# Cross-attention on one core: values of alternate head groups moved within their strip, output projection by two full products

## What is computed

```python
q = proj(hs, Wq, bq, S)          # 32 x 16 heads x 56 x 16
k = proj(at, Wk, bk, T)          # 32 x 16 heads x 1500 x 16
v = proj(at, Wv, bv, T)
scores = jnp.einsum('bhsd,bhtd->bhst', q, k) / scale
...
probs = jax.nn.softmax(scores, axis=-1)
ctx = jnp.einsum('bhst,bhtd->bhsd', probs, v)
ctx = ctx.transpose(0, 2, 1, 3).reshape(B, S, H)
delta = ctx @ Wo.T + bo
```

## Time and profile before

| | us |
|---|---|
| median of 3 runs | 1445.63 (1444.37 to 1446.39) |
| the profiled execution | 1444.34 |
| its span, first to last instruction | 1442.4 |
| PE busy | 1376.7 (95%) |
| PEld busy | 1176.8 (82%) |
| DVE busy | 1013.8 (70%) |
| ACT busy | 716.9 (50%) |
| POOL busy | 447.3 (31%) |

### The profile page before, as it was taken

One profiled execution on the slowest core, in us unless ns is written; L12 is line 12 of the kernel. 1 busy time (PEld: TensorE's weight loads), 2 busy tenths in 40 slices (PEclk: granted clock), 3 DMA queues, 4 the chain that ended last, 5 costly groups with the idle time before them and its releaser, 6 DMA issues.

```text
span 1442.4 us, 54968 instructions
## 1 busy us (share of the span) xinstructions
PE 1376.7 (95%) x25094; PEld 1176.8 (82%) x25094; DVE 1013.8 (70%) x1792; ACT 716.9 (50%) x939; POOL 447.3 (31%) x400
## 2 busy tenths in 40 slices
PE   5899999998899999999999999999999999999983
PEld 5687787786688888888888888888888888888872
DVE  4676676666136787786777777687878778677765
ACT  3445445444255645555555555555554555555540
POOL 4332333222222333333324233233333333332400
PEclk9999999999899999999999999999999999999995
DMA  9100001000111121111112121111212121121100
GB/s 260 23 1 31 1 1 31 1 30 1 58 49 57 31 77 44 56 58 46 58 37 63 31 77 52 57 49 45 64 31 77 41 62 55 45 61 34 49 2 7
DMA packets 38808, 66.75 MB, mean 46 GB/s; under 512 B 3605, under 2 KB 36818, under 8 KB 38578
## 3 DMA queue, kind: packets, MB, share of 16 engines
q1 hardware_dynamic: 38578, 63.24, 15.1%
HBM read 61.40 MB, written 1.84 MB: 44 GB/s over the span
## 4 chain that ended last, share of the span: by engine, by line
PE 71%; DVE 2%; issue 0%; POOL 0%; POOLq 0%; DVEq 0%
PE proj_ps L1277 19%; PE proj_ps L1268 19%; PE score_ps L1295 14%; PE sum_ps L1315 12%; PE side_ps L1350 2%; PE side_ps L1332 2%; PE side_ps L1364 1%; PE side_ps L1357 1%; PE side_ps L1339 0%; DVE inv L1109 0%; DVE exps L1097 0%; DVE amax L1150 0%; DVE hidden L1182 0%; DVE hidden L1193 0%; DVE sig L1192 0%
## 5 line engine op out<-in xcount | busy, mean ns | idle before, releaser
L1049 ACT ACTIVATE exps<-score_ps 125x1792 f32<-125x1792 f32 x192 | 320.5, 1669 | 419.0 <-PE score_ps L1295 419.0
L1097 DVE TENSOR_SCALAR exps<-exps,top 125x896 f32<-125x896 f32 x384 | 287.9, 791 | 18.0 <-ACT exps L1049 17.5
L1295 PE MATMUL score_ps<-spread,keys 32*125 32x112 f32 x6144 | 219.3, 279 | 0.0
L1315 PEld LDWEIGHTS sum_ps<-exps,vals 125*32 125x32 f32 x12288 | 163.0, 110 | 50.9 <-issue 34.4
L1088 DVE COPY vals<-proj_ps 125x512 f32<-125x512 f32 x192 | 128.2, 687 | 103.4 <-PE proj_ps L1277 103.0
L1295 PEld LDWEIGHTS score_ps<-spread,keys 32*125 32x125 f32 x6144 | 185.1, 183 | 15.4 <-issue 0.4
L1315 PE MATMUL sum_ps<-exps,vals 125*32 125x56 f32 x12288 | 191.5, 214 | 2.9 <-DVE exps L1097 2.9
L992 POOL TENSOR_TENSOR low<-raw_early,high 128x500 fp32r<-128x500 f32 x64 | 100.8, 1583 | 231.2 <-issue 115.4
L992 POOL TENSOR_TENSOR low_early<-raw_early,high_early 128x500 fp32r<-128x500 f32 x62 | 104.3, 1691 | 172.3 <-issue 104.1
L1041 ACT ACTIVATE keys<-proj_ps,b_k 128x500 f32<-128x500 f32 x192 | 129.9, 677 | 52.4 <-PE proj_ps L1268 52.4
L286 POOL TENSOR_TENSOR swapped<-swapped,sin 128x448 f32<-128x448 f32 (+1 forms) x72 | 88.6, 1232 | 138.5 <-ACT swapped L507 138.5
(11 more groups left out here) (156 smaller groups left out, 2411.6 us busy)
## 6 DMA issues: line engine op xcount, KB each, us to landing
raw_early<-in_ctxT SPq DMA_DIRECT2D x64, 500.0 KB, 4.0
raw<-in_ctxT SPq DMA_DIRECT2D x32, 500.0 KB, 3.5
w_q<-in_attn_Wq SPq DMA_DIRECT2D x4, 512.0 KB, 8.1
w_o<-in_attn_Wo SPq DMA_DIRECT2D x1, 2048.0 KB, 21.5
out<-y_out SPq DMA_DIRECT2D x16, 112.0 KB, 1.9
rows<-in_x SPq DMA_DIRECT2D x1, 1344.0 KB, 16.8
raw_early<-in_ffn_gate_wT SPq DMA_DIRECT2D x1, 1024.0 KB, 9.6
raw_early<-in_ffn_val_wT SPq DMA_DIRECT2D x1, 1024.0 KB, 5.1
```

The lines of the kernel that those rows point to most:

```text
L1049: nc.scalar.activation(exps[t % 2][:, :, :, :].rearrange("p h r n -> p r h n"), score_ps[0:TILE, :, 0:2 * QW].rearrange("p r (h n) -> p r ...
L1097: nc.vector.tensor_scalar(tile, tile, LIMIT_LO, top[:, n, at:at + 1], ALU.max, ALU.min)\
L1295: ins = nc.tensor.matmul(score_ps[0:TILE, r, to:to + HE * S], keys[c % 2][32 * r:32 * r + 32, k, (at + half) * TILE:(at + half + 1) * TILE ...
L1315: ins = nc.tensor.matmul(sum_ps[32 * h:32 * h + VW, g, :], vals[c % 2][:, at + half, HJ * g + h, :], exps[t % 2][:, half, r, col:col + S], ...
```

## The change

For groups 1 and 3, `add_up` takes a window of `vals` that begins 16 columns earlier: the ones of the head before, then the values of its own head. Their sums of exponents then stand in the upper 16 rows of a strip (the first ones) and the weighted values in the 16 rows behind them. `divide` takes the reciprocal as before, shuffles the even groups from the second 16 rows and the odd groups from the first, multiplies all, sets the unwanted rows of the odd groups to zero with a mask column (`part`), multiplies the even groups by the other mask column and adds the odd ones, and adds the bias. So two groups share one column block of `heads`, now 128 full rows, and L1332 is two products over 128 rows in place of four, with a `w_xo` without zeros whose rows are ordered on the host. `divide` has seven instructions (and two loads of a shuffle mask) in place of four (and one), and an `EventSemaphore` instruction less; four of them work on 112 elements or less per row instead of 224. The bias and the weights come in by one DMA each and the mask by one (14 early DMAs instead of 19).

```diff
-N_EARLY = 11 + 2 * HJ
+N_EARLY = 14
...
-SWAP = [HD + n % HD for n in range(2 * HD)]
+FROM_HIGH = [HD + n % HD for n in range(2 * HD)]
+FROM_LOW = [n % HD for n in range(2 * HD)]
+DIVS = 6
...
-        self.b_v = sb("b_v", [P, HG])
-        self.w_xo = sb("w_xo", [P, HG, D])
+        self.b_v = sb("b_v", [P, HG // 2])
+        self.w_xo = sb("w_xo", [P, HG // 2, D])
+        self.part = sb("part", [P, 2])
...
-        for j in range(HJ):
-
-            pairs += [(self.b_v[32 * j:32 * j + HD, :], dram["xattn_bv"][j]),
-                      (self.w_xo[32 * j:32 * j + HD, :, :],
-                       dram["xattn_WoT"].rearrange("(a j d) n -> j d a n", a=HG, j=HJ)[j])]
+        pairs += [(self.b_v[:, :], dram["xattn_bv"]), (self.part[:, :], dram["c_part"]),
+                  (self.w_xo[:, :, :], dram["xattn_WoT"].rearrange("(a p) n -> p a n", p=P))]
...
-        heads = sb("heads", [P, HG, 2, S])
+        heads = sb("heads", [P, HG // 2, 2, S])
...
-                chain = Chain(dve, div_step, 6 * p + 3 * k)
+                chain = Chain(dve, div_step, DIVS * (2 * p + k))
                 chain(nc.vector.reciprocal(inv[:, k, :, :], sums[:, k, :, :]))
-                nc.vector.sem_inc(inv_ready, 1)
-                chain(nc.vector.stream_shuffle(inv[:, k, :, :].rearrange("p a s -> p (a s)"),
-                                               inv[:, k, :, :].rearrange("p a s -> p (a s)"), SWAP))
-                chain(nc.vector.tensor_tensor(heads[:, :, k, :], sums[:, k, :, :], inv[:, k, :, :], ALU.mult))
-                nc.vector.tensor_tensor(heads[:, :, k, :], heads[:, :, k, :],
-                                        b_v[:, :].unsqueeze(2).to_broadcast([P, HG, S]), ALU.add)\
+                chain.inc(nc.vector.stream_shuffle(inv[:, k, 0::2, :], inv[:, k, 0::2, :], FROM_HIGH))
+                chain(nc.vector.stream_shuffle(inv[:, k, 1::2, :], inv[:, k, 1::2, :], FROM_LOW))
+                chain(nc.vector.tensor_tensor(inv[:, k, :, :], sums[:, k, :, :], inv[:, k, :, :], ALU.mult))
+                chain(nc.vector.tensor_scalar(inv[:, k, 1::2, :], inv[:, k, 1::2, :], part[:, 1:2], None, ALU.mult))
+                chain(nc.vector.scalar_tensor_tensor(inv[:, k, 0::2, :], inv[:, k, 0::2, :], part[:, 0:1], inv[:, k, 1::2, :],
+                                                     ALU.mult, ALU.add))
+                assert chain.n == DIVS
+                nc.vector.tensor_tensor(heads[:, :, k, :], inv[:, k, 0::2, :],
+                                        b_v[:, :].unsqueeze(2).to_broadcast([P, HG // 2, S]), ALU.add)\
                   .then_inc(heads_ready, 1)
...
+            def value_and_ones(r, tile, head):
+
+                at = (tile * XH + head) * VW - (HD if head // HJ % 2 else 0)
+                return vals[r][:, :, :, :].rearrange("p t h v -> p (t h v)")[:, at:at + VW]
...
-                                sum_ps[32 * h:32 * h + VW, g, :], vals[c % 2][:, at + half, HJ * g + h, :],
+                                sum_ps[32 * h:32 * h + VW, g, :], value_and_ones(c % 2, at + half, HJ * g + h),
...
-                    for a in range(HG):
+                    for a in range(HG // 2):
                         ins = nc.tensor.matmul(side_ps[0:ROWS, 0:D], heads[:, a, :, :].rearrange("p k s -> p (k s)"),
-                                               w_xo[:, a, :], start=(a == 0), stop=(a == HG - 1))
+                                               w_xo[:, a, :], start=(a == 0), stop=(a == HG // 2 - 1))
...
+        "c_part": np.stack([row % (2 * HD) < HD, row % (2 * HD) >= HD], 1).astype(np.float32),
...
-        "xattn_WoT": a(L0_xattn_Wo).T, "xattn_bq": a(L0_xattn_bq).reshape(DC, P).T,
+        "xattn_WoT": a(L0_xattn_Wo).T.reshape(HG // 2, 2, HJ, HD, D).transpose(0, 2, 1, 3, 4).reshape(D, D), "xattn_bq": a(L0_xattn_bq).reshape(DC, P).T,
...
-        "xattn_bv": a(L0_xattn_bv).reshape(HG, HJ, HD).transpose(1, 2, 0), "xattn_bo": a(L0_xattn_bo), "xattn_gamma": a(L0_xattn_ln_gamma),
+        "xattn_bv": a(L0_xattn_bv).reshape(HG // 2, 2, HJ, HD).transpose(2, 1, 3, 0).reshape(P, HG // 2), "xattn_bo": a(L0_xattn_bo), "xattn_gamma": a(L0_xattn_ln_gamma),
```

More of the change, by code:

```diff
@@ L47 @@
 TOTALS = (3, 7, 11)
-N_EARLY = 11 + 2 * HJ
+N_EARLY = 14
+WEIGHTS_AT = 13
 TILE = 125
@@ L872, in block_b @@
         w_h, w_l, b_k, spread, top = early.w_h, early.w_l, early.b_k, early.spread, early.top
-        head_of, ident_h, b_v, w_xo, b_xo, res = early.head_of, early.ident_h, early.b_v, early.w_xo, early.b_xo, early.res
+        head_of, ident_h, b_v, w_xo, b_xo, res, part = (early.head_of, early.ident_h, early.b_v, early.w_xo,
+                                                              early.b_xo, early.res, early.part)
         ln_gamma, ln_beta, gate_b, val_b, out_b = early.ln_gamma, early.ln_beta, early.gate_b, early.val_b, early.out_b
@@ L922, in block_b @@
         div_step = sem("div_step")
-        inv_ready = sem("inv_ready")
         side_ready = sem("side_ready")
```

## The result

The changed kernel takes 1461.73 us (median of 4 runs, 1460.02 to 1462.42), the kernel before 1445.19 beside it, a ratio of 1.0111 (95% interval 1.0089 to 1.0132): 1.1% slower, clear of noise. The forecast was 1461.0.

What follows compares the result with a forecast made beforehand. TensorE's own instructions were taken to bound the second part. 15 pairs x 1.08 = 16.2, pair 0 0.4 less, last pair -0.5: +15.3 on 1444.34, 1459.6; plus 1.29 for the median, 1461.0 us; range 1442 to 1470.

Steps and rivals of the forecast that it cites:

- TensorE's saving: Projection L1332: four of eight weight-load passes go, 0.86 us saved per pair.
- Shifted windows, DMAs: Add-up and setup: windows starting 64 bytes off, fewer early DMAs, smaller memset and constants cost or save nothing.
- Length of `divide`: VectorE from the reciprocal's end: 1.44 us before, 2.04 taken after, so 0.6 longer each (0.5 to 0.8).
- The hold in the first `divide`: GpSimd's L992 holds the merge, then turns alternate; the second reciprocal starts 0.71 us later.
- B: Rival: neither the merge held nor L1154 late, TensorE's saving wins outright: -7.7 us, 1438; chance 0.14.
- C: Rival: the merge isn't held, but L1154 is: +3.9 us, 1449.5; chance 0.08.
- The wait for the heads: At the projection: heads ready 1.3 us later against 0.19 in hand, TensorE waits 1.1; net +0.25 per pair.
- The hold of L1154: Before `xq`: L1154 0.52 us later, 0.08 behind GpSimd's L992, is held; TensorE's L1339 waits 0.83 per pair.
- The last pair: Both `divide` add 0.6 us each, half of the half-clock projection saves 1.7: together -0.5.
- Pair 0: First pair of the second part: has more in hand, gives about 0.4 us less than the 1.08 per pair.
- A: Rival: the second hold doesn't come, L1154 still ahead of L992: +2.8 us, 1448.4; chance 0.20.
- D: Rival: second mask load waits for first shuffle, mask product falls behind L992's start, chain one turn back: 1468 us; chance 0.06.

Runs made afterwards that it cites:

- e1: The kernel before with two of the projection's four products left out, so part of the computation is missing: 1430.49 us, ratio 0.9905.
- e4: The kernel before with only the shifted windows of the odd groups in the add-up, output not the reference's: 1446.20 us, ratio 1.0009.
- e10: The changed kernel once more, unaltered: 1460.63 us, ratio 1.0107 to the kernel before.
- e3: The changed kernel with one instruction of 0.19 us less in each quantise step: 1446.84 us, ratio 1.0014 to the kernel before.
- e7: The kernel before with two idle clamp steps more in quantise_rows, 0.38 us together, ahead of L1154: 1443.53 us, ratio 0.9997.
- e8: The kernel before with three idle clamp steps more in quantise_rows, 0.56 us together, ahead of L1154: 1457.65 us, ratio 1.0089.
- e2: The changed kernel with its two projection products issued twice, same result, so without TensorE's saving: 1458.28 us, ratio 1.0104 to the kernel before.
- e5: The changed kernel without mask product, two scalar_tensor_tensor replacing mask product, merge and bias, everything computed: 1428.59 us, ratio 0.9897 to the kernel before.
- e6: The changed kernel with GpSimd's two L993 beside the first divide cut to 2 columns from 500, part of the computation missing: 1433.68 us, ratio 0.9921 to the kernel before.

## Why the prediction was right, step by step

- **TensorE's saving**: 0.86 per pair forecast. The projection took 0.74 as forecast, and e1 shows 0.87 on the period.
- **Shifted windows, DMAs**: nothing forecast, nothing found (e4; e10 for the first part).
- **Length of `divide`**: 0.6 longer forecast, bounds 0.5 to 0.8; it is 0.48 (reciprocal's end 521.25 to 523.17, 1.92, against 1.44), just under the lower bound. (Five of the seven instructions work on 112 elements, as the forecast's sum has them; the description of the change says four.) The middle was the wrong choice: the second mask load hides completely (the second shuffle starts 0.09 ahead of the first one's end), and the first shuffle starts 0.04 after the reciprocal. The merge, priced like a tensor_tensor of its size (0.275), took 0.33. The first error is the larger.
- **The hold in the first `divide`**: the merge was to be held although no row showed it of such an instruction: it was, 1.40 instead of 0.33. That it was the merge is partly luck: it was to come 0.17 behind GpSimd's instruction (1.46 against 1.29 after the reciprocal's end) and came 0.00 to 0.01 behind it, because the `divide` was priced too long. Pair 0 shows that with the merge ahead the bias is held instead, a case between the forecast and rivals B and C. The queue behind it ran as written: from the reciprocal's end (513.99) the bias ends at 3.95 (3.93 forecast) and the second `limit` at 5.38 (5.35). The second reciprocal starts 0.74 later in relation to the first (0.71).
- **The wait for the heads**: 1.1 forecast, 1.02 to 1.05 found, mostly by the 0.12 that the second `divide` was priced too long. Net +0.18 instead of +0.25.
- **The hold of L1154 (now L1158)**: forecast 0.08 behind L992, the step most in doubt; it is 0.09 behind, takes 1.32 (1.34), and TensorE waits 0.83 to 0.87 (0.83). The chain in between held too: L1140's successor is 0.55 late (0.52). The rule under it, that the two engines take turns by order of arrival, is too strong as a general one, as the L992 at 535.12 shows. e3, e7 and e8 show the threshold from both sides. That this distance doesn't depend on what the new instructions cost was the firm part of the step: in e2, where TensorE leaves the projection no sooner, the wait is absent with the same `divide`.
- **The last pair**: -0.5 forecast; pair 14 is +1.1 and what follows -0.7. Pair 0: +0.7 forecast, +0.8 found.
- **The rivals**: A falls with the 1.32 of L1158, B and C with the 1.40 of the merge, D with the mask product, which is over (515.24) before L993 begins (515.27).

The sum came out at 15.3 against 15.5. The terms erred in different directions (0.07 per pair too much for the heads; 0.09 too little elsewhere, of which 0.04 is the second wait by the weight loads and the other 0.05 isn't accounted for), so agreement to a microsecond is partly luck. The medians moved by 16.5, and the first part of the kernel alone varies by more than the difference.

## What to carry to other kernels

Work taken from the engine that bounds a kernel brings the others nearer behind it by just that much; before counting it as gained, follow the next engine through the queue until its next slack, and look where its instructions then meet GpSimd's. Where two engines hold each other up by order of arrival, a tenth of a microsecond can decide over a whole instruction, in either direction: here one instruction of 0.19 us was worth 13 to 14 us of time. And rows that only need to be made harmless can be made a known constant: the mask product was there to clear rows that held 1, a sum times its own reciprocal, and the bias could take it off.

## What the runs showed of the hardware

- A scalar_tensor_tensor with two SBUF inputs waits for a GpSimd tensor_tensor that began 0.00 to 0.01 us ahead of it: 1.40 us instead of 0.33. The Trainium skill, page "SBUF — State Buffer", section on the two separate sides of SBUF, says of a VectorE instruction with two SBUF inputs and a GpSimd one that reads SBUF that whichever starts first blocks the other for its whole length. The hold of 1.40 agrees.
- Which of the two goes first doesn't always follow the recorded starts: at 535.12 in the kernel before, an L992 recorded 0.05 us ahead of the first `limit` behind `xq` waits for two of them and takes 2.45 us instead of 1.26.
- Between two shuffles with different masks the mask load costs nothing: the second begins 0.09 us before the first one's end, as back-to-back instructions do.
- A scalar_tensor_tensor on 112 elements takes 0.33 where a tensor_tensor takes 0.27 and a tensor_scalar 0.28.
- A tensor_scalar that begins 0.05 us ahead of GpSimd's instruction keeps its 0.35 us (e7), and one 0.09 or 0.12 behind takes 1.32 (the changed kernel) or 1.29 (e8).
- TensorE's granted clock between 20 and 40 us of the kernel averaged 1.00 in one execution and 0.83 in another, with the same code in it but for a few DMAs; the first part took 442 us with 13.7 us at the lower level (e5, e10) and 451 with 34.1 (e6).
